# Two transformer layers in one kernel: the first attention's loops written out, its operands read in place, its last turn and the early loads preparing the second layer

## What is computed

```python
xn = _layernorm(x)
x = x + attn0(xn) + ffn0(xn)      # attn0: 16 heads of 64, causal, k and v through a latent of 128
xn = _layernorm(x)                # ffn0: 128 -> 352 -> 128, silu gate, blockwise fp4 rounding
x = x + attn1(xn) + ffn1(xn)      # attn1: 16 heads of 8, biases, relative-position bias, not causal
                                  # ffn1: 128 -> 512 -> 128, ternary weights, gelu, biases b1 and b2
```

## Time and profile before

| what | us |
|---|---|
| three runs: lowest, median, highest | 2328.78, 2330.8, 2331.32 |
| the profiled execution's own time | 2329.29 |
| its span, from the first to the last instruction | 2327.4 |
| PE busy, share of the span | 2166.9 (93%) |
| DVE busy | 1676.7 (72%) |
| ACT busy | 1368.0 (59%) |
| POOL busy | 152.1 (7%) |
| mean granted clock of TensorE, share of full speed | 0.987 |

### The profile page before, as it was taken

One profiled execution on the slowest core, in us unless ns is written; L12 is line 12 of the kernel. 1 busy time (PEld: TensorE's weight loads), 2 busy tenths in 40 slices (PEclk: granted clock), 3 DMA queues, 4 the chain that ended last, 5 costly groups with the idle time before them and its releaser, 6 DMA issues. The chain is left out here.

```text
span 2327.4 us, 47308 instructions
## 1 busy us (share of the span) xinstructions
PE 2166.9 (93%) x19395; PEld 1342.4 (58%) x19395; DVE 1676.7 (72%) x2110; ACT 1368.0 (59%) x2161; POOL 152.1 (7%) x285
## 2 busy tenths in 40 slices
PE   3599999999999999999999989999999999999998
PEld 2467666666667666666667656544444444444444
DVE  8677777777777777777777764777777777777770
ACT  4456555565656555565656544266666666666666
POOL 2301001010101001010101000200000000000000
PEclk8799999999999999999999999999999999999999
DMA  3100000000000000000000019311111111110000
GB/s 106 14 0 0 0 0 0 0 0 0 0 0 0 0 0 0 0 0 0 0 0 0 0 17 225 68 20 20 20 20 29 20 28 35 23 20 20 11 2 10
DMA packets 41105, 41.24 MB, mean 18 GB/s; under 512 B 21345, under 2 KB 33601, under 8 KB 40866
## 3 DMA queue, kind: packets, MB, share of 16 engines
q1 hardware_dynamic: 39842, 39.05, 8.0%
q10 hardware_dynamic: 1152, 0.64, 0.1%
HBM read 27.71 MB, written 11.70 MB: 17 GB/s over the span
## 5 line engine op out<-in xcount | busy, mean ns | idle before, releaser
L1576 DVE TENSOR_REDUCE nm_half<-slot 128x2 f32<-128x1024 f32 x512 | 606.4, 1221 | 163.1 <-PE slot L1357 118.0
L1559 ACT ACTIVATE pT<-slot 128x1024 f32<-128x1024 f32 x512 | 505.7, 1026 | 269.2 <-PE slot L1466 214.7
L848 ACT ACTIVATE prob<-slot,negmax 128x1024 f32<-128x1024 f32 (+6 forms) x448 | 316.8, 718 | 214.4 <-DVE negmax L906 139.0
L682 PE MATMUL slot<-k_hl,q_hl 64*128 64x512 f32 (+3 forms) x2560 | 355.7, 358 | 57.7 <-ACT prob L848 55.3
L682 PEld LDWEIGHTS slot<-k_hl,q_hl 64*128 64x128 f32 x2560 | 252.6, 185 | 101.7 <-ACT prob L848 74.9
L717 PEld LDWEIGHTS slot<-ident,prob 128*128 128x128 f32 x2304 | 254.1, 141 | 87.9 <-issue 61.9
L717 PE MATMUL slot<-ident,prob 128*128 128x128 f32 x2304 | 288.3, 275 | 0.0
L729 PE MATMUL yspace<-probT,v_sb 128*64 128x512 f32 (+3 forms) x1536 | 275.9, 494 | 0.0
L559 DVE COPY probT<-slot 128x768 f32<-128x768 f32 (+1 forms) x192 | 166.8, 869 | 150.4 <-PE slot L717 147.6
L1432 PE MATMUL yspace<-pT,v 128*32 128x512 f32 x2048 | 267.0, 603 | 1.6 <-ACT y_raw L1546 0.8
L829 ACT ACTIVATE probT<-slot 128x1024 f32<-128x1024 f32 x192 | 170.0, 886 | 143.7 <-PE slot L717 122.1
(11 more groups left out here) (234 smaller groups left out, 2512.5 us busy)
## 6 DMA issues: line engine op xcount, KB each, us to landing
qs<-q_hi SPq DMA_DIRECT2D x64, 64.0 KB
qs<-q_lo SPq DMA_DIRECT2D x64, 64.0 KB
ks<-k_hi SPq DMA_DIRECT2D x64, 64.0 KB
ks<-k_lo SPq DMA_DIRECT2D x64, 64.0 KB
x_tok<-in_L_attn_x_dram SPq DMA_DIRECT2D x4, 512.0 KB, 7.8
q_hi<-qk_out SPq DMA_DIRECT2D x4, 512.0 KB, 4.3
q_lo<-qk_out SPq DMA_DIRECT2D x4, 512.0 KB, 6.0
k_hi<-qk_out SPq DMA_DIRECT2D x4, 512.0 KB, 6.5
```

The costliest lines, as they stand in the source:

```text
L682: nc.tensor.matmul(own_ps[a][:, o:o + m], q_hl[hq][own, i * P:(i + 1) * P], k_hl[hk][own, o:o + m], start=(k == 0), stop=(k == 3 and o + m ...
L848: last = nc.scalar.activation(prob[a][:, p_at(i, 0, w)], ps[:, o:o + w], ACT.Exp, bias=negmax[:, i, a:a + 1], accum_out=sums[:, i, a:a + 1])
L1559: nc.scalar.activation(pT[hp][m % PT_DEEP][:, :, :], slot[at["x", n] % RING][:, :].rearrange("p (j t) -> p j t", t=BANK), ACT.Exp)\
L1576: nc.vector.tensor_reduce(nm_half[:, h, :, p * TPB + i], slot[pos % RING][:, :].rearrange("p (a t) -> p a t", t=BANK), AX.X, ALU.max, nega ...
```

## The change

- The 32 turns of block B are written out on PE and ACT too (`turns` is a Python loop). POOL does nothing there but the ternary weights: all seven staging copies, their buffers and the two semaphores are gone, and PE reads slices of `wkv_all`, `wq_all`, `latT`, `xnT`, `xqT` and `wo_all`.
- In the last turn (31) there is no next turn. Before, it made keys and queries that nobody read. Now its task `keys` is empty, and its task `queries` turns over the normalised batch 0 of layer 1. For this, DVE computes the last moments earlier in the turn, ACT takes the root in the turn, in the place of its copy of the keys, and DVE inverts it and normalises batch 0 into `xn_early` (the scratch of the ternary weights) in the place of `next_low` for k. ACT copies the turned tiles to `xnT` in the place of the q copy.
- Block D therefore begins with task Q of batch 0.
- Four of the six bias loads (`bqk` twice, `b1_col`, `bv_row`) are issued in block A, behind the weights, and ACT scales bq at the end of block A. The two for `bsum` stay in block D, on a semaphore of their own.

The diff, cut to its core:

```diff
@@ block A, SP
+                    sp.dma_start(bqk[:, 0:1], bq1.unsqueeze(1)).then_inc(cb_in, 16)
+                    sp.dma_start(bqk[:, 1:2], bk1.unsqueeze(1)).then_inc(cb_in, 16)
+                    sp.dma_start(b1_col[:, :], b1.rearrange("(k p) -> p k", p=P)).then_inc(cb_in, 16)
+                    sp.dma_start(bv_row[:, :], bv1.unsqueeze(0).broadcast_to([P, C])).then_inc(cb_in, 16)
@@ block A, end of ACT
+                    act.wait_ge(cb_in, 64)
+                    nc.scalar.activation(bqk[:, 0:1], bqk[:, 0:1], ACT.Copy, scale=HD1 ** -0.5).then_inc(bq_scaled, 1)
@@ block B, PE, ACT
-                    with eng.Fori(0, B) as b:
-                        with eng.Fori(0, PAIRS) as g:
-                            body(b, g, b * PAIRS + g)
+                    for it in range(TURNS):
+                        body(it // PAIRS, it % PAIRS, it)
@@ block B, POOL
-                    stage_in(0, 0, 0)
-                    stage_out(0)
...
-                    with pool.Fori(0, PAIRS - 1) as g:
-                        next_turn(0, g + 1, g + 1)
...
@@ block B, PE
-                        pe.wait_ge(staged_in, it + 2)
...
+                        if it == TURNS - 1:
+                            pe.nop().then_inc(full[TK % RING], 1)
+                            pe.nop().then_inc(free[TK % RING], 1)
+                            return
...
-                            last = nc.tensor.matmul(ps[:, h * BANK:(h + 1) * BANK], wk_s[:, :], lat_s[:, h * BANK:(h + 1) * BANK], start=True, stop=True)
+                            last = nc.tensor.matmul(ps[:, h * BANK:(h + 1) * BANK], wkv_all[:, g * P:(g + 1) * P], latT[:, b * T + h * BANK:b * T + (h + 1) * BANK],
...
+                            pe.wait_ge(xn_set, 1)
...
+                            for t in range(TPB):
+                                last = nc.tensor.transpose(ps[:, t * P:(t + 1) * P], xn_early[:, t * C:(t + 1) * C], ident[:, :])
...
-                            pe.wait_ge(staged_out, it + 1)
@@ block B, ACT, last turn
+                            act.wait_ge(moment_step, 2 * known)
+                            nc.scalar.activation(std2[:, 0:known], moments[:, 0:known, 1], ACT.Sqrt, bias=eps_col[:, 0:1]).then_inc(std_ready, 1)
...
+                            frees(nc.scalar.activation(xnT[:, 0:T], slot[TQ % RING][:, :], ACT.Copy), TQ)
@@ block B, DVE, last turn
+                        if it == TURNS - 1:
+                            freed(dve, it - 1, TO)
+                            moments_of(finished)
...
+                            nc.vector.reciprocal(rstd2[:, known], std2[:, known]).then_inc(rstd_set, 1)
+                            dve.wait_ge(rstd_set, 1)
+                            for t in range(TPB):
+                                op = nc.vector.tensor_scalar(xn_early[:, t * C:(t + 1) * C], x_tok[:, t, :], moments[:, t, 0:1], rstd2[:, t:t + 1], ALU.subtract, ALU.mult)
@@ block D
-                CT = [("T", 0), ("Q", 0), ("K", 0), ("T", 1), ...
+                CT = [("Q", 0), ("K", 0), ("T", 1), ...
...
-                    act.wait_ge(cb_in, 96)
-                    nc.scalar.activation(bqk[:, 0:1], bqk[:, 0:1], ACT.Copy, scale=HD1 ** -0.5).then_inc(bq_scaled, 1)
...
-                    inverse(1, slice(0, (B - 1) * TPB))
-                    normal(0)
                     normal(1)
```

More of the change, by code:

```diff
@@ L89, in two_layers @@
         std_ready = sem("std_ready")
+        b1_col = sb("b1_col", [P, FC])
+        bqk = sb("bqk", [P, 2])
+        bv_row = sb("bv_row", [P, C])
+        rstd2 = sb("rstd2", [P, TILES])
+        cb_in = sem("cb_in")
+        bq_scaled = sem("bq_scaled")
+        rstd_set = sem("rstd_set")
+        xn_set = sem("xn_set")
         L0 = ExitStack()
@@ L212, in _ @@
                     sp.dma_start(W2_raw[:, :], W2).then_inc(w1_in, 16)
+                    with nc.allow_non_contiguous_dma(reason="a bias to one value a partition, once"):
+                        sp.dma_start(bqk[:, 0:1], bq1.unsqueeze(1)).then_inc(cb_in, 16)
+                        sp.dma_start(bqk[:, 1:2], bk1.unsqueeze(1)).then_inc(cb_in, 16)
+                        sp.dma_start(b1_col[:, :], b1.rearrange("(k p) -> p k", p=P)).then_inc(cb_in, 16)
+                    sp.dma_start(bv_row[:, :], bv1.unsqueeze(0).broadcast_to([P, C])).then_inc(cb_in, 16)
                     sp.wait_ge(w_in, 64)
@@ L420, in two_layers @@
                 PT_BUFS = 4
[L421 to L424, removed]
                 q_hl = [sB(f"q_hl{r}", [P, T], F32R) for r in range(2)]
@@ L444, in two_layers @@
                 hqT = sB("hqT", [P, 3, P])
-                above = sB("above", [P, F])
-                below = sB("below", [P, F])
+                xn_early = sB("xn_early", [P, 2 * F])
+                above, below = xn_early[:, 0:F], xn_early[:, F:2 * F]
                 six = sB("six", [P, 6])
@@ L565, in _ @@
                 def _(pool):
[L567 to L584, removed]
                     def ternary(i):
@@ L646, in values @@
                             for k in range(TPB):
-                                last = nc.tensor.matmul(ps[:, k * P:(k + 1) * P], lat_s[:, k * P:(k + 1) * P], wv_s[:, :], start=True, stop=True)
+                                last = nc.tensor.matmul(ps[:, k * P:(k + 1) * P], latT[:, b * T + k * P:b * T + (k + 1) * P], wkv_all[:, HD + g * P:HD + (g + 1) * P],
+                                                        start=True, stop=True)
                             last.then_inc(full[TV % RING], 1)
@@ L651, in gates @@
                             ps = claim(it, TGU)
-                            nc.tensor.matmul(ps[:, 0:I], xq_s[:, :], wguT[:, 0:I], start=True, stop=True)
-                            nc.tensor.matmul(ps[:, BANK:BANK + I], xq_s[:, :], wguT[:, I:2 * I], start=True, stop=True).then_inc(full[TGU % RING], 1)
+                            nc.tensor.matmul(ps[:, 0:I], xqT[:, it * P:(it + 1) * P], wguT[:, 0:I], start=True, stop=True)
+                            nc.tensor.matmul(ps[:, BANK:BANK + I], xqT[:, it * P:(it + 1) * P], wguT[:, I:2 * I], start=True, stop=True).then_inc(full[TGU % RING], 1)
                         def score_claim(n):
@@ L763, in project @@
                                 for t in range(4 * c, 4 * c + 4):
-                                    last = nc.tensor.matmul(ps[:, t * P:(t + 1) * P], y_sb[:, t * P:(t + 1) * P], wo_s[:, :], start=True, stop=True)
+                                    last = nc.tensor.matmul(ps[:, t * P:(t + 1) * P], y_sb[:, t * P:(t + 1) * P], wo_all[:, g, :], start=True, stop=True)
                             last.then_inc(full[TO % RING], 1)
@@ L865, in body @@
                         hidden()
-                        next_high(it, TQ, q_hl)
+                        if it < TURNS - 1:
+                            next_high(it, TQ, q_hl)
+                        else:
+                            filled(act, it, TQ)
+                            frees(nc.scalar.activation(xnT[:, 0:T], slot[TQ % RING][:, :], ACT.Copy), TQ)
                     turns(act, body)
-                    known = (B - 1) * TPB
-                    act.wait_ge(moment_step, 2 * known)
-                    nc.scalar.activation(std2[:, 0:known], moments[:, 0:known, 1], ACT.Sqrt, bias=eps_col[:, 0:1]).then_inc(std_ready, 1)
                 @blockB.vector
@@ L954, in body @@
                         freed(dve, it - 1, TO)
-                        if finished is not None:
+                        if finished is not None and it < TURNS - 1:
                             moments_of(finished)
@@ L1095, in two_layers @@
                 c_at = {task: n - len(CT) - 2 * MU - XT for n, task in enumerate(CT)}
-                AHEAD = (2 * MU + XT + len(CT) + 2) // RING
-                assert len(CT) == 4 * B and (2 * MU + XT + len(CT) + 2) % RING == 0
+                AHEAD = (2 * MU + XT + len(CT)) // RING
+                assert len(CT) == 4 * B - 1 and (2 * MU + XT + len(CT)) % RING == 0
                 FREE1 = 1
@@ L1292, in _ @@
                 def _(pe):
-                    for s in range(2):
-                        pe.nop().then_inc(full1[s], 1)
                     for _ in range(AV0):
@@ L1322, in up @@
                     def up(t, f):
-                        if f == 0 and t % 2 == 0:
+                        if f == 0 and t % 2 == 0 and t:
                             ring_freed(pe, 0, c_at["T", t // 2])
@@ L1648, in _ @@
                     normal(3)
-                    for kind, b in CT[3:]:
+                    for kind, b in CT[2:]:
                         if kind == "V":
```

65 lines of the change are left out of this document (30 added, 35 removed).

## The result

| what | before | changed |
|---|---|---|
| median of the runs (lowest to highest), us | 2329.26 (2328.01 to 2331.44), 10 runs | 2323.49 (2321.79 to 2326.56), 10 runs |
| ratio to before | | 0.9975, interval 0.9965 to 0.9985 |
| profiled execution's own time; span, us | 2329.29; 2327.4 | 2324.25; 2322.4 |
| mean turn of block B, from gates to gates, us | 40.29 | 40.46 |
| POOL busy, us | 152.1 | 47.5 |

What follows compares the result with a forecast made beforehand. PE, busy 93% of the span, was taken as the bound, with block B's turns already tight. Gains of 2.8, 0.5 and 10.1 us summed to 13.4 us, giving a 2317 us median; range 2307 to 2323 us.

Steps and rivals of the forecast that it cites:

- Written-out turns: Block B's turns on PE and ACT: dropping staging waits and loop register work was put at 0 us.
- The bounds for registers: Loop register work in block B: taken as 0, at most 54 us gained; the range kept 0.3 us a turn, 10 us.
- Operands in place, copies gone: Block B: POOL's 3.26 us of copies a turn cost PE nothing, and reading slices of longer tiles gains 0.
- ACT's table load hidden: Block B: the 1.28 us table load in every turn of ACT's loop is hidden, so removing it gains 0.
- Code loading: Rival, block B on PE: fetching written-out code falls behind; one exposed 4.49 us fetch a turn gives 2461 us; chance 0.03.
- loop branches: Rival, block B: each of 31 loop edges held a 4.49 us fetch, so writing out gives 2178 us; chance 0.01.
- The rival of registers that cost tenths of a microsecond: Block B: 0.1 to 0.3 us a turn of waits on ACT go, 3 to 10 us more gained; chance 0.10.
- Start of block B: PE's first keys start when POOL's staging did, less ACT's 0.20 us scaling: gain 2.8 us, ends 1.0 and 4.6.
- Last turn: Turn 31 of block B: missing keys and shorter queries, against later DVE work, gain 0.5 us; ends 0 and 2.9.
- Seam of block D: From block B's last projection into block D: a shorter PE stop and a higher clock gain 10.1 us.
- the stop: Start of block D: task Q starts 1.7 us behind PE's end instead of 9.62 us, gain 7.9 us.
- the clock: Start of block D: PE stays at 2.4 GHz, Q and K take 3.5 us instead of 5.75, gain 2.2 us.

Runs made afterwards that it cites:

- e1: The kernel before with only PE's 32 turns of block B written out, ACT's and POOL's loops kept: 2335.48 us, 1.0021 of before, turns of 40.45 us.
- e9: The kernel before with PE's turns written out and the first score tile's slot asked for first: 2328.81 us, 0.9999 of before, turns of 40.29 us.
- e10: e3 with the seven staging copies a turn back on POOL, into scratch tiles nobody reads: 2319.89 us, 0.9956 of before, turns of 40.30 us.
- e2: The kernel before with only ACT's 32 turns of block B written out: 2329.80 us, 1.0000 of before, turns of 40.29 us.
- e11: The changed kernel run a second time, unaltered: 2323.98 us, 0.9979 of before, turns of 40.47 us.
- e3: The changed kernel with PE asking first for the first score tile's slot, which DVE frees last: 2319.27 us, 0.9949 of before, turns of 40.30 us.
- e5: e3 with PE's pv_done and av_done semaphore instructions moved behind the first work of blocks B and D: 2318.33 us, 0.9948 of before.

## Why the prediction was wrong, and where it was right

- **Written-out turns: the step that failed.** "The waits were satisfied long before", so the term was 0. That is true of the waits for staged operands that were taken out. It left out the waits that stayed: their number is the same, but as constants they are compiled into another order, in which the critical one stands first in an instruction of its own. Measured: +5.35 us between the profiles, +0.17 us a turn; e1 has it alone and e9 undoes it. The bounds for registers ran from 0 to a gain, and I had put no end below nothing, though no reason excluded one. What should have warned is the edge itself. The earlier trace rows show only PE there, and "no gap" was read from the projection's modelled end. With DVE's row beside it, as shown above, its subtraction ends at 295.05 + 1.22 = 296.27 us and PE's first scores start at 296.35 us: release and start met to within 0.1 us, so anything put behind that wait would show in full.
- **Operands in place, copies gone: 0.** Held; e10 has them back at no cost that can be told. DVE's 0.09 us on `eg` does not reach PE. The Trainium skill (SBUF — State Buffer, "SBUF: two separate sides") would explain it, and the traces agree in sign: the add takes 0.33 us in all turns of the changed kernel, and 0.37 us in the turns of e10 that have copies.
- **ACT's table load hidden: 0.** Held; e2.
- **Code loading and loop branches.** Neither rival shows: the turns of the changed kernel agree within 0.03 us, and e9's are the loop's. The rival of registers that cost tenths of a microsecond does not show either, on ACT (e2) or on PE (e9). The Trainium skill (Runtime: NRT & Kernel Launch, "Instruction fetch mechanics") says that a taken branch to code outside the loaded window stalls, and that kernels therefore prefer full unrolling. For PE's loop unrolling gained nothing: with the source's order of waits it is 0.21% slower (e1), with the new order the same (e9). No run shows whether the loop's branch left the loaded window, so this is no test of the stall itself.
- **Start of block B: 2.8 forecast.** From block A's last transposes to the first keys it was 4.76 us and is 2.91 us: 1.85 us. The missing 1 us is PE's seven increments, 0.15 us each, which were hidden behind POOL's copies. The prediction let PE start when POOL did. At the gates the gain is 1.17 us in the first profile and nothing in e11 (23.83 us against 23.43), where the clock was low for longer. Besides the keys' 1.85 us, 0.4 us went to queries at a lower clock (2.29 us against 1.88) and 0.2 us to the waits ahead of turn 0. The 1.17 us are inside the ends of 1.0 to 4.6 us, e11's are not.
- **Last turn: 0.5 forecast, 1.08 measured.** The copy of item 7 came after DVE's normalisation, and PE waited for it, as worked out, but it came only 0.8 us late against the gates and not 1.5 us. So PE was 0.19 us ahead of its old time at the queries, where 0.5 us behind was forecast, and won 0.89 us by the shorter task. These rows of the changed kernel answer to the earlier trace rows:

```profile
1375.03 2.14 DVE L954 TENSOR_SCALAR xn_early<-x_tok,moments,rstd 128x128 f32<-128x128 f32 x8
1377.71 0.42 DVE L567 COPY probT<-slot 128x256 f32<-128x256 f32 x1
...
1378.19 1.31 PE L714 MATMUL slot<-ident,prob 128*128 128x128 f32 x10 [0.36 <-DVE probT L567]
```

- **Seam of block D: 10.1 forecast, 7.8 measured.** The terms were the stop, 7.9 us, and the clock, 2.2 us. Q starts 2.18 us behind PE's last work, not 1.7, since PE's four increments stand ahead of it: 7.4 us of the 7.9. DVE did begin 1.68 us behind PE's end, as forecast. The clock's term came out near nothing in this execution (5.37 us against 5.73, 0.4 us) and nearly in full in e11 (3.67 us, 2.1 us), whose seam is 12.15 us long, 9.45 us less than before. "With a stop of 1.7 us PE should stay at 2.4 GHz" was a term with two outcomes, priced as one.

**The sum.** Between the profiled executions 13.4 us were forecast and 5.0 us came, a miss of 8.4 us. The turns are 5.35 us of it, the seam of block D 2.3 us and the start of block B 1.6 us; against that, the last turn gave 0.6 us more than forecast, and the stretches that nobody forecast gave 0.3 us. With the order of waits put right, the change has e3's 2319.3 us, inside the forecast's own range of 2313 to 2321 us. So what the prediction said of the seams stands as a mechanism, with sizes that were too large by the increments and the clock. What failed is the zero for the written-out turns: writing out could cost by the order of waits, and the prediction's only case for a cost, code loading, is not what happened.

e3 and e5 beat both kernels: 0.9949 and 0.9948 of before, where the changed kernel has 0.9975.

## What to carry to other kernels

When an engine waits for several things at one point, see to it that in the compiled program the wait that will end last rides on the instruction itself, with everything else ahead of it, and look at this order again whenever a loop is written out. The order of the source does not tell it: in the written-out turns the wait that the program asked for first was the one that came to ride on the matmul (the high parts in the changed kernel, slot 0 in e3). Before costing an edit near a critical hand-over at nothing, read how far apart release and start are: where they meet within 0.1 us, there is no cover. A small gain that rests on the clock staying up after a stop should be booked as a chance of that gain, and medians of several executions are needed to see it.

## What the runs showed of the hardware

- What stands behind the critical wait costs PE, by the semaphore records, 0.11 us for the second semaphore instruction and 0.075 us for the matmul's own wait, though both were satisfied: together 0.19 us, where the turns of e1 and of the changed kernel are 0.17 us longer. An instruction that only increments a semaphore costs PE 0.15 us.
- The granted clock behind a stop of some 2 us is not the same from one execution to the next: 0.50 and 1.00 were both seen with stops of 2.19 and 2.22 us. It is worth 1.3 to 1.7 us for one task at each of three places, and 2.8 us between the kernel before and e2 over the whole start of block B. The scatter between executions of one kernel (4.8 us for the changed one) could come from there, which is not shown, since only the profiled executions tell the clock by place.
- The hardware loop's edge cost nothing that can be seen in block B: 40.29 us a turn with it on PE and 40.29 us without (e9).
